# A routed feed-forward layer: the experts' tiles gather rows by token lists and add into the output, with both shared passes ahead of them

## What is computed

```python
x = x + xattn(layernorm(x), ctx)      # per batch: quantised x (128-blocks) times quantised ctx, transposed
h = layernorm(x)
scores = sigmoid(h @ gate_w)          # 32 experts in 4 groups; the best 2 groups, then the best 6 experts
weights = picked / sum(picked)
d[t, k] = (silu(h @ w_gate[e]) * (h @ w_up[e])) @ w_down[e]     # e = the k-th expert of token t, inner width 704
shared = (silu(h @ sw_gate) * (h @ sw_up)) @ sw_down            # inner width 1408
out = x + sum_k d[t, k] * weights[t, k] + shared
```

## Time and profile before

| | |
|---|---|
| median of 3 runs | 6813.99 us (6783.92 to 6828.12) |
| the profiled execution | 6804.45 us, its span 6802.6 us |
| mean granted TensorE clock | 0.976 |
| busy, share of the span | PE 94%, POOL 47%, DVE 25%, ACT 17% |
| moved by DMA | 1191.37 MB, 175 GB/s on average |

### The profile page before, as it was taken

One profiled execution on the slowest core, in us unless ns is written; L12 is line 12 of the kernel. 1 busy time (PEld: TensorE's weight loads), 2 busy tenths in 40 slices (PEclk: granted clock), 3 DMA queues, 4 the chain that ended last, 5 costly groups with the idle time before them and its releaser, 6 DMA issues.

```text
span 6802.6 us, 89488 instructions
## 1 busy us (share of the span) xinstructions
PE 6366.1 (94%) x32176; PEld 3144.9 (46%) x32177; DVE 1686.7 (25%) x2601; ACT 1177.3 (17%) x1769; POOL 3164.6 (47%) x2117
## 2 busy tenths in 40 slices
PE   2999999927999999999999999999999999998899
PEld 1555544413444444444444444444444444444444
DVE  7888432000111111111111111111111111115556
ACT  3666521100111111111111111111111111110000
POOL 4444504456444564444654456444564466443222
PEclk9999999968999999999999999999999999999999
DMA  2555637995555565555655556555565566559898
GB/s 94 175 178 176 205 94 266 358 338 167 143 143 140 152 168 154 143 143 148 165 156 152 141 150 170 156 148 143 153 166 154 141 166 173 142 148 247 243 265 241
DMA packets 1154501, 1191.37 MB, mean 175 GB/s; under 512 B 868368, under 2 KB 870416, under 8 KB 1153936
## 3 DMA queue, kind: packets, MB, share of 16 engines
q10 hardware_dynamic: 902064, 476.87, 29.1%
q1 hardware_dynamic: 187872, 487.28, 21.7%
q0 software_dynamic: 64512, 226.53, 10.6%
HBM read 663.88 MB, written 343.93 MB: 148 GB/s over the span
## 4 chain that ended last, share of the span: by engine, by line
PE 76%; DMA 8%; DVE 6%; issue 5%; POOL 3%; ACT 2%; ACTq 1%; DVEq 0%; POOLq 0%; SPq 0%
PE ps_gu L747 49%; PE ps_d L747 23%; PE ps_d L950 3%; DMA rows_x<-wts,slot_now 2%; DMA wts<-rows_x 2%; DMA wts<-rows_d 1%; DMA out<-wts 1%; DMA hT<-hid_hl 1%; POOL rows_x L677 1%; ACT wts L1103 1%; DVE wts L1443 1%; DVE wts L1593 1%; DMA rows_x<-wts,pad_now 1%; DVE max_rows L1374 0%; DVE amax L1370 0%
## 5 line engine op out<-in xcount | busy, mean ns | idle before, releaser
L747 PE MATMUL ps_gu<-wts,xT 128*128 128x512 f16 (+1 forms) x20304 | 3959.7, 356 | 220.7 <-DVE hid L1563 163.4
L747 PEld LDWEIGHTS ps_gu<-wts,xT 128*128 128x128 f16 x20304 | 1996.4, 98 | 2149.7 <-issue 231.5
L747 PE MATMUL ps_d<-wts,hT 128*128 128x512 f16 x7938 | 1768.7, 381 | 37.6 <-DMA hT<-hid_hl 37.4
L559 POOL TENSOR_SCALAR wts<-stage 128x1408 f16<-128x1408 f32 (+3 forms) x483 | 586.6, 1214 | 2169.1 <-PE ps_d L950 2134.0
L1563 DVE SCALAR_TENSOR_TENSOR hid<-ps_gu,sil 128x704 f32<-128x704 f32 (+2 forms) x272 | 234.0, 860 | 4377.8 <-ACT sil L1224 4377.8
L562 POOL TENSOR_TENSOR wts<-stage,wts 128x1408 f16<-128x1408 f32 (+3 forms) x482 | 1227.8, 2547 | 40.2
L747 PEld LDWEIGHTS ps_d<-wts,hT 128*128 128x128 f16 x7938 | 778.3, 98 | 970.8 <-DMA hT<-hid_hl 34.6
L1224 ACT ACTIVATE sil<-ps_gu 128x704 f32<-128x704 f32 (+2 forms) x272 | 199.1, 732 | 2710.0 <-PE ps_gu L747 2568.6
L560 POOL TENSOR_SCALAR stage<-stage 128x1408 f32<-128x1408 f32 (+3 forms) x483 | 621.9, 1287 | 0.0
L1245 ACT ACTIVATE dout<-ps_d 128x1024 f32<-128x1024 f32 x240 | 245.6, 1023 | 2105.5 <-DMA xT<-xin 1984.1
L747 PE MATMUL ps_d<-wts,xin 128*128 128x512 f16 x1536 | 351.0, 383 | 18.4 <-DVE xin L1394 14.0
(11 more groups left out here) (176 smaller groups left out, 2210.8 us busy)
## 6 DMA issues: line engine op xcount, KB each, us to landing
rows_d<-dout ACTq DMA_DIRECT2D x240, 512.0 KB, 3.2
xin<-rows_x ACTq DMA_DIRECT2D x211, 512.0 KB, 3.3
stage<-in_L_ffn_w_down SPq DMA_DIRECT2D x384, 256.0 KB, 3.2
stage<-in_L_ffn_w_gate SPq DMA_DIRECT2D x256, 352.0 KB, 3.2
stage<-in_L_ffn_w_up SPq DMA_DIRECT2D x256, 352.0 KB, 3.8
wts<-in_x SPq DMA_DIRECT2D x64, 512.0 KB, 3.9
rows_x<-wts SPq DMA_DIRECT2D x64, 512.0 KB, 3.3
wts<-rows_x SPq DMA_DIRECT2D x64, 512.0 KB, 6.1
```

Source lines behind the costliest of these rows:

```text
L559: g.tensor_scalar(high, raw, WSCALE, 1.0, ALU.mult, ALU.mult).then_inc(conv_step, 1)
L747: ins = nc.tensor.matmul(dst[c], left, right[c], start=(first and a == 0), stop=(last and a == 2))
```

## The change

Both shared passes now come before the experts, and the experts work directly on the output.

- GpSimd no longer scatters rows. For each pair of token and expert it writes 8 bytes, the token's number and its routing weight, into a list in DRAM (`list_rows`); SP loads the sorted list once into SBUF (`lists`). The routing arithmetic changes to give list addresses. The padding is a preset number out of range.
- Pass A's product is added to `rows_x1` by GpSimd with an accumulating transfer (`add_down`) instead of being stored by ACT. Two token tiles' list entries follow each of these from tile 9 on (`LIST_FROM`, `LISTS_A_TILE`).
- Pass B follows pass A. Its weights are split by VectorE beside pass A's tiles 14 to 26. Its `take_down` adds to `rows_x1`'s row, and SP stores the output. The combine, `rows_d` and the spare copies go.
- For an expert tile GpSimd gathers its rows by the list (`gather_x`), gathers the same tokens' output rows (`gather_y`), adds the tile's product to them (`add_y`; ACT applies the routing weight on eviction) and scatters them back to the output. The next tile's `gather_y` waits until that has landed.
- VectorE splits expert weights with two instructions a piece instead of three (expert 0's stay on GpSimd). In its place GpSimd multiplies silu by up and makes the low part; ACT first copies the up half out of PSUM (`take_up`).
- TensorE's `gate_up` of an expert tile waits for ACT's two reads of PSUM instead of for `hid_done`.

```diff
-                spare_tile(i)
...
-            with sp.Fori(1, TT // 2) as q:
-                for u in range(2):
-                    sp.wait_ge(scat_out[u], q * (16 * TOPK))
-                    sp.dma_start(xsc[u], rows_x[ds((q * 2 + u) * P, P), :]).then_inc(xsc_in[u], 16)
+            sp.wait_ge(lists_clear, 1)
+            sp.dma_start(list_rows.rearrange("(p j) c -> p (j c)", p=P),
+                         lists[:, 0:SLOT_TILES, :].rearrange("p j c -> p (j c)")).then_inc(lists_blank, 16)
...
-            with sp.Fori(0, E // 2) as q:
-                for u in range(2):
-                    mats = [w[ds(q * 2 + u, 1)].rearrange("a r c -> (a r) c") for w in (w_gate, w_up, w_down)]
...
             for c in range(CHUNKS_B):
-                sp.wait_ge(conv_done, E // 2 * PAIR + piece(EVEN, c) - STAGES + 1)
-                load_half(EVEN, c, AT_B, MB)
-
+                sp.wait_ge(conv_done, piece(HALF_B, c) - STAGES + 1)
+                load_half(HALF_B, c, AT_B, MB)
+            for c in range(STAGES):
+                load_expert(FIRST, c, slice(0, 1))
+            sp.wait_ge(list_out, 16 * TOPK * TT)
+            sp.dma_start(lists[:, 0:SLOT_TILES, :].rearrange("p j c -> p (j c)"),
+                         list_rows.rearrange("(p j) c -> p (j c)", p=P)).then_inc(lists_in, 16)
...
+            sp.wait_ge(conv_done, chunks_before[FIRST])
+            for u in range(2):
+                sp.wait_ge(d_out, 16 * u + 16)
+                side(u, u)
+            for i in range(TT):
+                if i < CHUNKS - STAGES:
+                    load_expert(FIRST, i + STAGES, slice(0, 1))
+                elif i < CHUNKS:
...
+            with sp.Fori(0, E // 2 - 1) as q:
                 for u in range(2):
-                    store_out(q * 2 + u, u)
-                    sp.wait_ge(o_out, q * 64 + 32 * (u + 1))
+                    for c in range(CHUNKS):
+                        load_expert(EVEN + u, c, ds(q * 2 + (u + 2), 1), q)
...
-            with pool.Fori(0, TT // 2) as q:
-                    for k in range(TOPK):
-                        g.indirect_dma_start(
-                            out=rows_x, out_offset=bass.IndirectOffsetOnAxis(ap=slot_now[:, u, k:k + 1], axis=0),
...
+            def add_down(n):
+                pool.wait_ge(d_free, n + 2)
+                pool.wait_ge(s_added, n * 16 + 16)
                 pool.sem_inc(pool_turn, 1)
+                g.dma_start(rows_x1[ds(n * P, P), :], dout[:, :], accum_op=ALU.add).then_inc(d_out, 16)
+
+            def list_tile(t):
+
+                        out=list_rows, out_offset=bass.IndirectOffsetOnAxis(ap=slot[:, t, k:k + 1], axis=0),
+                        in_=pairs[:, t, k, :], in_offset=None, bounds_check=P * SLOT_TILES - 1,
...
+            for n in range(1, TT):
+                add_down(n)
+                if n == LIST_FROM:
+                    pool.wait_ge(slots_ready, 1)
+                    pool.wait_ge(lists_blank, 16)
+                        list_tile(t)
+            pool.wait_ge(conv_done, chunks_before[FIRST])
+            pool.wait_ge(down_done, TT)
+            for c in range(CHUNKS):
+                split_piece(FIRST, c, 0)
...
+            def gather_x(n, free):
+                if free:
+                    pool.wait_ge(xt_in, n * 16)
+                g.tensor_copy(x_now[:, :], lists[:, ds(r, 1), 0:1].rearrange("p a c -> p (a c)")).then_inc(x_index, 1)
+                g.indirect_dma_start(out=xin[:, :, :].rearrange("p a d -> p (a d)"), out_offset=None, in_=rows_x,
+                                     in_offset=bass.IndirectOffsetOnAxis(ap=x_now[:, 0:1], axis=0),
...
+            def gather_y(r, first=False):
+                if not first:
+                    pool.wait_ge(y_out, r * 16)
+                g.tensor_copy(y_now[:, :], lists[:, ds(r, 1), 0:1].rearrange("p a c -> p (a c)")).then_inc(y_index, 1)
+                pool.wait_ge(y_index, r + 1)
+                g.indirect_dma_start(out=y_rows, out_offset=None, in_=o_rows,
+                                     in_offset=bass.IndirectOffsetOnAxis(ap=y_now[:, 0:1], axis=0),
...
+            def add_y(r):
+                pool.wait_ge(d_free, r + (TT + 2))
+                pool.wait_ge(y_in, r * 16 + 16)
+                g.tensor_tensor(y_rows, y_rows, dout[:, :], ALU.add).then_inc(y_sum, 1)
+                g.indirect_dma_start(out=o_rows, out_offset=bass.IndirectOffsetOnAxis(ap=y_now[:, 0:1], axis=0),
+                                     in_=y_rows, in_offset=None, bounds_check=T - 1,
+                                     oob_is_err=False).then_inc(y_out, 16)
...
+            def hidden(n):
+                pool.wait_ge(up_done, n - (N_R - 1))
+                g.tensor_tensor(hid_flat[:, 0:M], hid_flat[:, 0:M], sil_flat[:, 0:M], ALU.mult).then_inc(hid_done, 1)
+            def low_of_hidden(n):
+                pool.wait_ge(hid_high, n + 1)
+                g.tensor_tensor(hid_hl[:, M:M + M_LAST], hid_flat[:, K_LAST:M], hid_hl[:, K_LAST:M], ALU.subtract)
+                g.tensor_tensor(hid_hl[:, M + M_LAST:], hid_flat[:, 0:K_LAST], hid_hl[:, 0:K_LAST],
+                                ALU.subtract).then_inc(hid_low, 1)
+
+            def tile(n, second=False):
+
+                gather_y(n - (N_R + 1), first=second)
+                hidden(n)
+                low_of_hidden(n)
+                add_y(n - (N_R + 1))
+                gather_x(n + 3, free=True)
...
+            pool.wait_ge(o_out, 32 * TT)
+            tile(N_R + 1, second=True)
+            with pool.Fori(N_R + 2, N_ALL) as n:
+                tile(n)
...
+            pe.wait_ge(weights_ready, 2)
+            tile_b(TT, 0, None, before=down_a)
+            pe.wait_ge(d_free, TT + 1)
+            tile_b(TT + 1, 1, None)
...
-                pe.wait_ge(hid_done, n)
+                if start == 0:
+                    pe.wait_ge(hid_done, n)
+                else:
+                    pe.wait_ge(up_done, n - N_R)
+                    pe.wait_ge(silu_done, n)
...
-                    before(n - 1, 1 - u)
+                    pe.wait_ge(d_free, n - TT)
+                by_buffer(down, n - 1, buf_before, 1 - u)
...
-            def store_d(n):
+            def evict(n):
-                act.wait_ge(d_out, n * 16 + 16)
...
-                act.wait_ge(d_free, n + 2)
-                act.dma_start(rows_d[ds(n * P, P), :], dout[:, :]).then_inc(d_out, 16)
...
+            def evict_weighted(n, r, first=False):
+                else:
+                    act.wait_ge(y_sum, r)
+                a.activation(dout[:, :], ps_d_flat, ACT.Copy,
+                             scale=lists[:, ds(r, 1), 1:2].rearrange("p a c -> p (a c)").bitcast(F32)).then_inc(d_free, 1)
+            def take_up(n):
+                a.activation(hid_flat[:, 0:M], ps_gu_flat[:, M:2 * M], ACT.Copy,
+                             scale=HSCALE / WSCALE).then_inc(up_done, 1)
...
-            def tile(n):
-
-                hidden(n, M, ps_gu_flat[:, M:2 * M])
...
+            def split_piece(o, c, buf, pair=0, m=M):
+                dve.wait_ge(stage_in[st], pair * PAIR_LANDED + landed(o, c))
+                v.tensor_scalar(high, raw, WSCALE, 1.0, ALU.mult, ALU.mult).then_inc(cast_done, 1)
+                dve.wait_ge(cast_done, pair * PAIR + cast_of(o, c))
+                v.scalar_tensor_tensor(out=low, in0=raw, scalar=WSCALE, in1=high, op0=ALU.mult,
+                                       op1=ALU.subtract).then_inc(conv_done, 1)
...
+                v.tensor_scalar(pairs[:, :, :, 1].bitcast(F32), top_w[:, :, :], 1.0 / (WSCALE * HSCALE), None, ALU.mult)
+                v.tensor_copy(pairs[:, :, :, 0], token[:, :].unsqueeze(2).to_broadcast([P, TT, TOPK]))
...
+            dve.wait_ge(s_dn, TT)
+            for n in range(B_FROM, TT):
+                tile_a(n)
+                if n < B_FROM + CHUNKS_B:
+                    split_piece(HALF_B, n - B_FROM, 1, m=MB)
+                if n == B_FROM + CHUNKS_B:
+                    dve.wait_ge(conv_done, chunks_before[FIRST])
...
+            dve.wait_ge(o_out, 32 * TT)
+            dve.wait_ge(down_done, N_R)
+            for c in range(CHUNKS):
+                split_piece(SECOND, c, 1)
...
+            with dve.Fori(0, E // 2 - 1) as q:
+                for u in range(2):
+                    dve.wait_ge(down_done, done)
+                    for c in range(CHUNKS):
+                        split_piece(EVEN + u, c, u, q)
```

More of the change, by code:

```diff
@@ L17 @@
+import itertools
 from contextlib import ExitStack
@@ new lines, in _ @@
+            hidden(N_R)
+            low_of_hidden(N_R)
+            gather_x(N_R + 3, free=True)
+            pool.wait_ge(o_out, 32 * TT)
+            pool.wait_ge(d_out, 16 * TT)
+            tile(N_R + 1, second=True)
+            with pool.Fori(N_R + 2, N_ALL) as n:
+                tile(n)
+            with pool.Fori(N_ALL, N_MAX) as n:
+                with pool.If(n < n_tiles):
+                    tile(n)
+            r_last = pool.value_load(count_tab[0:1, 1:2], min_val=FULL - 1, max_val=SLOT_TILES - 1)
```

(42 more changed lines are left out.)

500 lines of the change are left out of this document (186 added, 314 removed).

## The result

The changed kernel takes 6588.05 us (median of 4 runs, 6575.98 to 6601.9) against 6814.18 (6783.92 to 6828.12): a ratio of 0.9675, interval 0.9637 to 0.9712. The forecast was 6545, its range 6505 to 6690. The profiled execution took 6590.12, its span 6588.2.

What follows compares the result with a forecast made beforehand. TensorE's work plus a few waits bounds the kernel. 1408.3 + 5.2 + 622.4 + 4492.4 = 6528.3 us, plus 9 for the tail, 6 for the lists and 1.9 beyond the span, gives 6545; range 6505 to 6690.

Steps and rivals of the forecast that it cites:

- The main case: Whole kernel: faster, at the forecast time of 6545 us, own range 6510 to 6600, chance 0.68.
- The gap: Between pass A and the experts: TensorE's waits of 129.6 and 38.4 us go, with two pass A tiles remaining, 31.1 us.
- Lists: GpSimd in pass A: twelve small scatters at 1.28 us follow each add, a round of 16.6 against 15.54, costing 6 us.
- Rival 2: Pass A: list scatters at 1.99 us each hold it up by 136 us, giving 6681; chance 0.05.
- VectorE's split: Experts' weights: VectorE splits one expert in 34 to 71 us, fitting into 108, so it costs nothing.
- Round trip: Expert tiles: scatter to the output until the next gather lands, 11.6 to 20.4 us, under the tile's 21.6.
- Rival 5: Expert tiles: the round trip through the output sets the tile at 24.1 us, slower, 7065; chance 0.08.
- the second cover of the experts: GpSimd's list per expert tile: about 11 of 21.6 us, so the work fits under TensorE's products.
- the 13 us said to be left behind the add: Expert tiles: slack after `add_y` for the eviction behind it, before TensorE needs the PSUM, 13 us.
- rival 1: Expert tiles: VectorE and GpSimd get in each other's way, 95 us over 31 experts, giving 6640; chance 0.11.
- the tail of 9: After the last product: eviction 1.2, add 2.1, wait 0.9, scatter to landing 4.5, together 9 us.
- Rivals 3 and 4: Pass B keeps 22.9 us a tile, 6655, chance 0.05; the gap moves before the experts, 6713, chance 0.03.

## Why the prediction was right, and where it was off

The main case came true: faster, inside the range. The gap and pass B are right to a few us. The gap of 168 us in two waits went and did not come back elsewhere; pass B lost 105 us and runs at 19.45 a tile; between the passes no wait of TensorE is over 3.5 us. The one of 3.44, for an eviction at pass B's start, and the slower product behind it (14.84 for 13.14) are 5.1 of the 5.5 us in the table's second row, and no term of the forecast. The late expert tiles took 28 of the 40 us that the forecast's range left for late lists and held instructions. The 19 us at the end were in no allowance, and the 8 us gained at the start hid part of them.

*Start.* 8.3 us better, inside the 10 that were left as a possible gain of the spare copies. Which part of the edits gives it was not tried.

*Lists.* Priced at 1.28 us each from below; the page's group of them (busy, mean, idle before) gives (196.7 + 57.0) / 192 = 1.32:

```profile
L652 POOL DMA_INDIRECT list_rows<-pairs,slot x192 | 196.7, 1024 | 60.1 <-issue 57.0
```

The delay was forecast at 6 and is 5.9, at the end of the list tiles, as the slack of 16 us said. Rival 2 is out.

*VectorE's split.* From 3812.37 to 3853.5, 41 us an expert where 34 to 71 was the bound. Nothing waits for it.

*Round trip.* An add at 6535.27, the next gather of output rows at 6543.13, landing 4.2 later: 12.1 us, near the lower end of 11.6 to 20.4. Rival 5 is out.

**The step that failed** is the second cover of the experts: "Together about 11 of 21.6 us", and with it the 13 us said to be left behind the add. GpSimd's own list was not far off: 12 us in an undisturbed tile (21.6 less 9.7 of waits for others, 6525.35 to 6546.95) and 13 on average. (Of its arithmetic the prediction says that rows agree with a factor of about two between the engines; its own rows give 1.4 to 1.6, and here 640 columns take 1.40 us on GpSimd, 1.7 times VectorE's 0.82.) But the limit is the circle through ACT, 18.5, which the prediction did not add up. One tile of this circle, and then a tile beside VectorE's split, in the timeline of the changed kernel:

```profile
3795.59 2.36 POOL L701 TENSOR_TENSOR s_out<-s_out,dout 128x1024 f32<-128x1024 f32 x1 [5.55 <-ACT dout L1262]
...
3799.90 0.20 POOL L681 COPY x_now<-lists 128x1 int32 x1
3800.99 1.05 POOL L684 DMA_INDIRECT xin<-rows_x,x_now  x1 [0.90 <-POOL x_now L681]
...
3806.48 1.67 POOL L711 TENSOR_TENSOR hid<-hid,sil 128x704 f32<-128x704 f32 x1 [2.00 <-ACT hid L1266]
...
3810.88 1.29 ACTq L1246 DMA_TRANSPOSE hT<-hid_hl  x1
...
3812.36 2.30 ACTq L1228 DMA_TRANSPOSE xT<-xin  x1
...
3814.97 1.11 ACT L1262 ACTIVATE dout<-ps_d,lists 128x1024 f32<-128x1024 f32 x1 [5.92 <-issue]
...
3816.24 3.36 POOL L701 TENSOR_TENSOR s_out<-s_out,dout 128x1024 f32<-128x1024 f32 x1 [5.45 <-ACT dout L1262]
3817.31 3.04 DVE L1594 TENSOR_SCALAR wts<-stage 128x1408 f16<-128x1408 f32 x1
...
3822.85 1.62 DVE L1596 SCALAR_TENSOR_TENSOR wts<-stage,wts 128x1408 f16<-128x1408 f32 x1
3822.94 1.57 POOL L681 COPY x_now<-lists 128x1 int32 x1
...
3825.41 2.45 POOL L684 DMA_INDIRECT xin<-rows_x,x_now  x1 [0.90 <-POOL x_now L681]
...
3840.89 5.26 ACTq L1228 DMA_TRANSPOSE xT<-xin  x1
...
3846.45 1.11 ACT L1262 ACTIVATE dout<-ps_d,lists 128x1024 f32<-128x1024 f32 x1 [11.06 <-issue]
...
3860.17 17.36 PE L766 MATMUL ps_gu<-wts,xT 128*128 128x512 f16 x72 [4.70 <-DMA xT<-xin]
```

In the first tile the eviction follows the transposes at once, and the add follows the eviction. Beside the split each of GpSimd's steps loses 1.0 to 1.4 us (add 3.36 for 2.36, copy 1.57 for 0.20, issue 2.45 for 1.05), and VectorE's cast 2.2 (3.04 for 0.89). The product with silu comes at 3832.81 where 3806.48 + 21.6 = 3828.1 would be in time. Then a transpose is issued for 5.26 us, the eviction comes 9.9 late (3846.45, against 3814.97 + 21.6), and TensorE waits 4.70 for the rows.

That such delays cost 28 us in all and not ten times as much is because each is repaid: a down needs its PSUM only some 10 us after the usual eviction starts (3794.32 to 3804.71), and the circle gains 3.1 back in each tile that follows.

This is rival 1 in part: the two engines do get in each other's way, by 1.0 to 1.4 us per instruction where it assumed 1.77. Its price of 95 us was too high, and its cause is not enough: held instructions without loads cost 1.6 us in all. The Trainium skill describes the holding (SBUF — State Buffer, "SBUF: two separate sides": the shared port pair belongs to one engine for its whole instruction). The trace agrees to 0.04 us: the copy begun at 3822.94 ends at 3824.51, VectorE's subtraction at 3824.47. The held issues of indirect transfers, which no row of before showed, are there as well.

*The end* was forecast 19 us too short, in two places. The last down waits 5.2 us and then takes 9.9 for products that take 7.5 elsewhere: no gate-up product is left to cover the way to it. The eviction that frees its PSUM ends at 6555.49 + 1.11 = 6556.60, 3.9 after the product before the wait. The other 1.3 no row assigns. And the tail of 9 is 20.5:

```profile
6555.49 1.11 ACT L1262 ACTIVATE dout<-ps_d,lists 128x1024 f32<-128x1024 f32 x1 [5.97 <-issue]
...
6560.02 1.03 POOL L704 DMA_INDIRECT out<-s_out,y_now  x1 [0.91 <-POOL s_out L701]
...
6570.15 0.18 POOL L691 COPY y_now<-lists 128x1 int32 x1 [6.96 <-issue]
...
6578.57 1.02 POOL L704 DMA_INDIRECT out<-s_out,y_now  x1 [0.92 <-POOL s_out L701]
```

The last gather of output rows is issued only behind that copy, 10.1 us after the scatter before it and not 3.5 as in the loop, so its round trip stands after the last product; the forecast had only the second half. The 6.96 us have no cause in the timeline, which leaves branches out, but GpSimd's own branch records show one. The kernel has room for 224 tiles, and from the 193rd on its loop tests whether the tile exists (L743). For the 16 that don't, GpSimd makes 16 empty turns of 0.43 us. Behind the last scatter stands a closing instruction of GpSimd (L110) of 5.96 us, which the forecast did not have either. The records of these two lines from 6560 on:

```profile
L743 POOLq COMPARE_BRANCH  x16: 50/50/55, 6562.2 to 6568.7; - x16
L110 POOLq DRAIN  x1: 5957/5957/5957, 6582.0 to 6582.0; - x1
```

No run tried the kernel without the empty turns. By the timeline they cost up to 6.2 us: the last add starts at 6575.31, and the eviction that it needs ended at 6569.09.

*Rivals 3 and 4* are out: pass B keeps no part of its old pace, and no gap stands before the experts. "What slowed it is gone" was right for a reason that it did not give: two causes, and removing either gives back most of the loss.

The fourth tile, late by 1.6 to 8.6 us in every profile but that of the repeated changed kernel (0.9), and the split moved back to GpSimd were not tried by themselves.

## What to carry to other kernels

The slack of an engine is not its idle time. Where two in-order lists wait for each other, follow one piece of work around until it meets itself, waits included, and compare that length with the period; lengthening one list by a known amount measures it. And a step that gets faster sends its transfers off faster: the split that was moved to the quicker engine cost little by itself, and what it cost came through the loads that it released, so pacing it by tiles gave the time back. Last, write out what stands behind a loop's last full turn by itself, empty turns included: here it took 19 us more than forecast, 0.3% of the time.

## What the runs showed of the hardware

- The issue of a DMA transpose on ACT, 2.3 us at the median, took up to 18.2 in the run without the split, where loads of 352 KB followed each other, and up to 23.4 with the earlier eviction (median 2.0). ACT started nothing else meanwhile.
- TensorE's 30 products of a down took 6.64 us where no wait stood before them, 9.01 behind a wait of 5.18 in the changed kernel and 8.16 behind one of 9.52 in the kernel before. In the run with GpSimd's longer list, where 204 downs wait 5.8 us on average, the mean granted clock was 0.926, against 0.992.
- An empty turn of a guarded loop took GpSimd 0.43 us, in which the timeline shows nothing.
- GpSimd's indirect scatter of 128 rows takes 1.02 us to issue whether a row has 8 bytes or 4 KB (0.97 in the earlier trace rows).
